# Second layer normalisation written by ScalarE instead of VectorE, and the gate's first step one slot earlier

## The chip, the cores and the metric

One core of a Trainium2 chip runs the whole program. The time is the device time of one execution in microseconds (us); lower is better. The engines are TensorE (PE; its weight loads are shown apart as PEld), VectorE (DVE), ScalarE (ACT), GpSimd (POOL) and the queue engine SyncE (SP). Each runs its own instructions in order, and they wait for one another on semaphores.

## What is computed

2048 rows (tokens) of 128 numbers pass an attention over the context and then a mixture of experts. The reference, cut to what matters:

```python
def layernorm(x): return (x - mean(x)) / sqrt(var(x) + 1e-5)      # along a row

# attention: Wq gives queries, keys and values; 32 x 64 rows are read as one batch of rows
q = layernorm(x) @ Wq.T;  k = v = ctx @ Wq.T
x1 = x + softmax(causal(q @ k.T / sqrt(128))) @ v

# mixture of 8 experts (128 -> 256 -> 128), the two with the highest gate each
xf = layernorm(x1)
gates = softmax(xf @ gate_W)
cw = the two highest gates of a row, scaled to the sum 1; 0 for the others
out = xf + sum over e of cw[:, e] * (relu(xf @ W1[e] + b1[e]) @ W2[e] + b2[e])
result = x1 + out
```

The second layer normalisation, `xf = (x1 - mean) * rstd` with `rstd = (var + 1e-5) ** -0.5`, is what the change touches. In the kernel x1 has a row in each partition, so mean and rstd are one number for each partition and tile.

## The kernel before

**Tiling.** The 2048 rows are 16 tiles of 128 rows, in 4 groups of 4 tiles (groups 0 to 3). The four passes of the main loop, `group(g)`, run the 8 experts over group g, two slots for each expert: slot 2e and slot 2e+1 of pass g. In this document the passes are called first, second, third and fourth (g = 0 to 3). Inside the slots of pass g stands the attention and the gate of the next group, g+1 (and the first half of the attention of g+2), so that group g+1 is ready when its pass begins. The work ahead of the loop (here "the head") does the attention and the gate of group 0 in two halves of two tiles and begins group 1.

**One pass.** In each step e PE first multiplies expert e+1's first layer (`hidden_product`: two column blocks c = 0 and 1, 3 matmuls of 512 columns each, into psH0 and psH1; products of fp16 halves `hi` and `lo`), then does the work of slot 2e, then expert e's second layer (`output_product`, into psY0 or psY1 by turns), then slot 2e+1. ACT follows with `hidden_relu`: for each of psH0 and psH1 an fp16 result h_hi and an fp32 result h (experts 0 and 3 only h). POOL and DVE subtract them for h_lo (`hidden_lo0` for the first block, `hidden_lo` for the second). DVE adds each expert's output, times the gate, to acc (`add_expert`, 4 instructions at L864). A bank psH is free for the next expert when ACT has written its h; a bank psY is free when DVE has added it.

**Order.** A table of numbers gives each helper step the slot of its engine; `run(steps, slot)` calls a step of group a in slot `(a - 2) * 16 + at` of the whole loop, which for steps of group g+1 is slot `at - 16` of pass g. All engines' lists are written out in that order when the program is built. The chain that the change touches, for group g+1 in pass g:
- slot 5: DVE's `variance_step` (statistics of x1, var2), POOL's `attention_rstd` (rstd2, a power of -1/2)
- slot 7 (NORM2 = 23): DVE's `second_norm`, 4 instructions at L784 that write xf
- slot 10 (26): PE transposes xf into psB (`xf_transposes`, L292), ACT evacuates it as fp16 x_hi (`x_hi_part`, L548), DVE writes the rest x_lo (`x_lo_part`, L790), POOL sums x1 and xf into acc (`base_sum`)
- slot 12 (28): PE's `logit_product` (12 small matmuls, L354 to L356, into psD), which waits for x_lo
- slot 13 (29): DVE's `gate_top` (L800 to L808: the logits, the highest of them, `below` = logits less the highest), then ACT's `gate_exps` (exp of below, L553)
- slots 14 and 15: DVE's `gate_choice` and `gate_weights` (L814 to L839).

In the pass that is at expert 7 PE multiplies expert 0 of the next group, and ACT's `hidden_relu` for it stands right behind `gate_exps` in ACT's order. The next `hidden_product` on PE waits for that `hidden_relu`.

In the head the same steps of group 0 run once in halves: DVE's `second_norm` between the statistics of group 1's x and their mean; ACT's `values_out` of group 1 (L527) and then `x_hi_part` (L548); PE's transposes of xf, the score product of group 1 (L333) and the first `hidden_product` in halves (L506 to L508); DVE's mask and maximum of group 1's scores (L741), w1_lo, and `gate_top`.

Of the kernel before, what the change touches and what calls it, by code (L numbers as in the profile page):

```python
# [7 lines left out]
ALU = mybir.AluOpType  # L8
ACT = mybir.ActivationFunctionType
# [24 lines left out]
def xattn_moe(nc, x, ctx, wq, gate_w, w1, b1, w2, b2, out):  # L34
    P = 128
# [4 lines left out]
    TG = 4  # L40
# [30 lines left out]
    with stack:  # L71
        def sb(name, shape, dt=fp32):
            return stack.enter_context(nc.sbuf_tensor(name, shape, dt))
# [4 lines left out]
        def sem(name):  # L78
            return stack.enter_context(nc.semaphore(name))
# [51 lines left out]
        x1 = sb("x1", [P, TG, D])  # L131
        stats2 = sb("stats2", [P, TG, 6])
        mv2 = sb("mv2", [P, TG, 2])
        var2 = sb("var2", [P, TG])
        rstd2 = sb("rstd2", [P, TG])
        xf = sb("xf", [P, TG, D])

        logits = sb("logits", [P, TG, E])
# [28 lines left out]
        LOOP_BANKS = {"xT": psA, "ctxT": psC, "keysT": psB, "values": psC, "scores": psA, "probsT": psB, "attn": psA,  # L167
                      "xfT": psB}
# [4 lines left out]
        ALL = range(TG)  # L173
        HALVES = list(zip((range(0, 2), range(2, 4)), HEAD_BANKS))
# [26 lines left out]
        attn_ps = sem("attn_ps")  # L201
        x1_ready, var2_ready, rstd2_ready = sem("x1_ready"), sem("var2_ready"), sem("rstd2_ready")
        xf_ready, xfT_ps, xhi_ready, xlo_ready = sem("xf_ready"), sem("xfT_ps"), sem("xhi_ready"), sem("xlo_ready")
        base_ready = sem("base_ready")
# [21 lines left out]
        X_OUT, KEYS_OUT, VALUES_OUT, EXPS, PROBS_OUT, X_HI, GATE_EXP = 11, 13, 15, 16, 18, 26, 29  # L226
        STATS, MAX, RESIDUAL, VARIANCE, NORM2, X_LO, GATE_TOP, CHOICE, WEIGHTS = 11, 15, 20, 21, 23, 26, 29, 30, 31
        W1_LO = (3, 0, 2, 5)
# [289 lines left out]
        def _(act):  # L518
# [16 lines left out]
            keys_halves_out = evacuate(keysT, "keysT", keysT_ps, keysT_ready, 1.0 / (SK * SV))  # L535
# [9 lines left out]
            def x_hi_part(a, ts, banks):  # L545
# [3 lines left out]
                                     scale=SX).then_inc(xhi_ready, len(ts))  # L549

            def gate_exps(a):
                act.wait_ge(below_ready, a + 1)
                nc.scalar.activation(gate_exp[:, :, :], below[:, :, :], ACT.Exp).then_inc(gate_exp_ready, 1)  # L553
# [20 lines left out]
            def inputs_out(a):  # L574
# [3 lines left out]

            steps = [(X_OUT, 2, inputs_out), (KEYS_OUT, 2, lambda a: keys_halves_out(a, ALL, LOOP_BANKS)),
                     (VALUES_OUT, 2, lambda a: values_halves_out(a, ALL, LOOP_BANKS)),  # L580
# [52 lines left out]
            keys_out(1, ALL, FIRST_BANKS)  # L633
            values_out(1, ALL, FIRST_BANKS)
            for ts, banks in HALVES:
                x_hi_part(0, ts, banks)
# [88 lines left out]
        def _(dve):  # L725
# [54 lines left out]

            def second_norm(a, ts):
                for t in ts:
                    dve.wait_ge(rstd2_ready, a * TG + t + 1)
                    nc.vector.tensor_scalar(xf[:, t, :], x1[:, t, :], mv2[:, t, 0:1], rstd2[:, t:t + 1],  # L784
                                            ALU.subtract, ALU.mult).then_inc(xf_ready, 1)

# [111 lines left out]
            def wq_lo_part():  # L898
                dve.wait_ge(wq_hi_ready, 2)
                for whole, hi, lo in ((gram, gram_hi, gram_lo), (wqT, wqT_hi, wqT_lo)):  # L900
# [3 lines left out]
            steps = [(CTX_LO, 2, ctx_lo_part), (STATS, 2, statistics), (MAX, 2, lambda a: mask_and_max(a, ALL, banks_of(a))),  # L904
                     (RESIDUAL, 1, residual_step), (VARIANCE, 1, variance_step), (NORM2, 1, lambda a: second_norm(a, ALL)),
                     (X_LO, 1, lambda a: x_lo_part(a, ALL, LOOP_BANKS)), (GATE_TOP, 1, lambda a: gate_top(a, chain)),
# [87 lines left out]
            for ts, banks in HALVES:  # L994
                second_norm(0, ts)
            chain.wait()
# [36 lines left out]
```

## Time and profile before

| | us |
|---|---|
| median of 3 runs (131.57 to 131.89) | 131.86 |
| the profiled execution | 130.83 |
| span of its trace | 129.0 |

| engine | busy us | share of the span | instructions |
|---|---|---|---|
| PE matmul | 120.3 | 93% | 1175 |
| PE weight load | 90.7 | 70% | 1175 |
| DVE | 107.6 | 83% | 419 |
| ACT | 93.5 | 73% | 191 |
| POOL | 53.5 | 41% | 57 |

The granted clock of PE is 1.00 over the whole span (2.4 GHz). The main loop begins at about 21.4 us; the passes end at about 51, 79, 105 and 126.6 us. Busy time counts an instruction from its start to its end, and neighbours on one engine overlap a little; a matmul of 512 fp16 columns lasts 0.38 us and the next one starts 0.22 us after it. So PE's starts tell more than its busy share: where a start comes later than the one before it plus the usual step, PE has lost that time.

### The profile page before, as it was taken

Reading aid. Unit: us, or ns where it says so; the run is one execution under the profiler, and the core shown is the slowest. Engines: PE = TensorE matmul, PEld = TensorE weight load, DVE = VectorE, ACT = ScalarE, POOL = GpSimd, SP = SyncE. Lnnn points to the kernel's source line nnn. Section 1 sums busy time; section 2 is a strip of 40 time slices with the busy share of each in tenths; the row PEclk is TensorE's granted clock in tenths of the full one; section 3 lists DMA queues with packets and bytes.
Section 4 is the critical chain, followed back from the end, with each engine's and each line's share of the span. In section 5 each row is a group of like instructions: output and inputs, shape, how many; then the busy total and the mean of one; then the engine's idle time right before and its main releaser. Section 6 shows DMA issues by size and latency. Waiting matters only on the chain. (4 is left out here: it accounts for less than half of the span.)

```text
span 129.0 us, 3295 instructions
## 1 busy us (share of the span) xinstructions
PE 120.3 (93%) x1175; PEld 90.7 (70%) x1175; DVE 107.6 (83%) x419; ACT 93.5 (73%) x191; POOL 53.5 (41%) x57
## 2 busy tenths in 40 slices
PE   6987788999979999999999999999999979999991
PEld 2585566777847768778768778778776757776690
DVE  0629998989999999989898999958998798866683
ACT  3337485999776955996779927993799467989830
POOL 7199155330094951330095640330468303345400
PEclk9999999999999999999999999999999999999999
DMA  3999900000000000200000000200000002000002
GB/s 92 321 283 321 289 26 8 0 0 0 5 0 0 0 5 3 81 0 5 0 0 5 0 3 13 68 5 0 3 0 8 0 0 86 3 0 0 5 0 81
DMA packets 9904, 5.54 MB, mean 43 GB/s; under 512 B 504, under 2 KB 9888, under 8 KB 9888
## 3 DMA queue, kind: packets, MB, share of 16 engines
q1 hardware_dynamic: 9744, 5.27, 15.2%
q8 instruction: 9, 0.15, 0.5%
q10 hardware_dynamic: 144, 0.07, 0.2%
q14 instruction: 7, 0.06, 0.1%
HBM read 4.28 MB, written 1.05 MB: 41 GB/s over the span
## 5 line engine op out<-in xcount | busy, mean ns | idle before, releaser
L690 POOL TENSOR_TENSOR h_lo<-h,h_hi 128x512 f16<-128x512 f32 x24 | 28.7, 1196 | 40.2 <-ACT h L571 39.9
L571 ACT ACTIVATE h<-psH,b1T 128x512 f32<-128x512 f32 x64 | 43.3, 689 | 1.1 <-PE psH L508 0.9
L570 ACT ACTIVATE h_hi<-psH,b1T 128x512 f16<-128x512 f32 x48 | 33.0, 688 | 11.5 <-PE psH L387 11.4
L864 DVE SCALAR_TENSOR_TENSOR acc<-psY,weight_y,acc 128x128 f32<-128x128 f32 x125 | 35.1, 342 | 1.4 <-PE psY L408 1.2
L383 PE MATMUL psH<-x_hi,w_hi 128*128 128x512 f16 x62 | 23.5, 379 | 1.0 <-ACT h L571 1.0
L387 PE MATMUL psH<-x_lo,w_hi 128*128 128x512 f16 x62 | 23.5, 379 | 0.0
L384 PE MATMUL psH<-x_hi,w_lo 128*128 128x512 f16 x62 | 23.5, 379 | 0.0
L848 DVE TENSOR_TENSOR h_lo<-h,h_hi 128x512 f16<-128x512 f32 x24 | 16.5, 689 | 7.8 <-ACT h L571 7.3
L408 PE MATMUL psY<-w_hi,h_hi 128*128 128x128 f16 x192 | 22.7, 219 | 0.0
L408 PE MATMUL psY<-w_lo,h_hi 128*128 128x128 f16 x192 | 22.7, 219 | 0.0
L408 PEld LDWEIGHTS psY<-w_hi,h_hi 128*128 128x128 f16 x192 | 15.3, 98 | 2.2
L408 PE MATMUL psY<-w_hi,h_lo 128*128 128x128 f16 x192 | 14.6, 219 | 0.8 <-POOL h_lo L690 0.8
L408 PEld LDWEIGHTS psY<-w_sb,h 128*128 128x128 f32 x116 | 14.1, 192 | 1.0
L408 PEld LDWEIGHTS psY<-w_lo,h_hi 128*128 128x128 f16 x192 | 14.7, 98 | 0.0
L408 PE MATMUL psY<-w_sb,h 128*128 128x128 f32 x116 | 14.3, 275 | 0.0
L673 POOL TENSOR_TENSOR rstd<-var,half 128x4 f32<-128x4 f32 (+1 forms) x5 | 4.7, 953 | 21.8 <-DVE var L771 21.8
L408 PEld LDWEIGHTS psY<-w_hi,h_lo 128*128 128x128 f16 x192 | 11.6, 98 | 1.0 <-issue 0.9
L387 PEld LDWEIGHTS psH<-x_lo,w_hi 128*128 128x128 f16 x62 | 6.1, 98 | 7.3
L383 PEld LDWEIGHTS psH<-x_hi,w_hi 128*128 128x128 f16 x62 | 6.1, 98 | 6.9 <-ACT h L571 3.1
L384 PEld LDWEIGHTS psH<-x_hi,w_lo 128*128 128x128 f16 x62 | 6.1, 98 | 2.8
L677 POOL TENSOR_TENSOR rstd<-mv,half 128x4 f32<-128x4 f32 x4 | 5.0, 1250 | 5.8 <-DVE mv L734 5.8
L682 POOL TENSOR_TENSOR acc<-x,xf 128x512 f32<-128x512 f32 x4 | 7.1, 1784 | 0.0
(191 smaller groups left out, 191.4 us busy)
## 6 DMA issues: line engine op xcount, KB each, us to landing
w_sb<-in_L_ffn_W_dram SPq DMA_DIRECT2D x8, 256.0 KB, 4.9
out_dram<-acc SPq DMA_DIRECT2D x3, 256.0 KB, 2.3
x_sb<-in_x_dram SPq DMA_DIRECT2D x2, 256.0 KB, 4.0
ctx_sb<-in_ctx_dram SPq DMA_DIRECT2D x2, 256.0 KB, 4.4
x_sb<-in_x_dram SPq DMA_DIRECT2D x1, 512.0 KB, 7.6
ctx_sb<-in_ctx_dram SPq DMA_DIRECT2D x1, 512.0 KB, 8.5
out_dram<-acc SPq DMA_DIRECT2D x2, 128.0 KB, 1.8
wq_sb<-in_L_xattn_Wq_dram ACTq DMA_DIRECT2D x1, 64.0 KB, 2.8
```

Of the source, the lines that this page charges most:

```text
L383: nc.tensor.matmul(psH[c][:, :], w1_hi[:, e, w], x_hi[:, g, :], start=True, stop=False)
L384: nc.tensor.matmul(psH[c][:, :], w1_lo[:, e, w], x_hi[:, g, :], start=False, stop=False)
L387: nc.tensor.matmul(psH[c][:, :], w1_hi[:, e, w], x_lo[:, g, :], start=False, stop=True).then_inc(z_ps, 1)
L408: last = nc.tensor.matmul(o, hidden[:, C * i + c, t * P:(t + 1) * P], weights[:, e, c, :], start=start and c == 0, stop=stop and c == C - 1)
L570: nc.scalar.activation(h_hi[:, C * (e % 2) + c, :], psH[c][:, :], ACT.Relu, bias=bias, scale=scale)
L571: nc.scalar.activation(h[:, C * (e % 2) + c, :], psH[c][:, :], ACT.Relu, bias=bias, scale=scale).then_inc(h_ready, 1)
L673: nc.gpsimd.tensor_tensor(rstd2[:, v], var2[:, v], half[:, v], ALU.pow).then_inc(rstd2_ready, len(ts))
L677: nc.gpsimd.tensor_tensor(rstd[:, bass.ts(a, TG)], mv[:, bass.ts(a, TG), 1], half[:, 0:TG], ALU.pow).then_inc(rstd_ready, TG)
L682: nc.gpsimd.tensor_tensor(acc[:, bass.ts(a, TG), :], x1[:, :, :], xf[:, :, :], ALU.add).then_inc(base_ready, 1)
L690: nc.gpsimd.tensor_tensor(h_lo[:, i, :], h[:, i, :], h_hi[:, i, :], ALU.subtract).then_inc(hlo0_ready, 1)
L848: nc.vector.tensor_tensor(h_lo[:, i, :], h[:, i, :], h_hi[:, i, :], ALU.subtract).then_inc(hlo_ready, 1)
L864: last = nc.vector.scalar_tensor_tensor(out=o, in0=y, scalar=weight_y[:, g % 2, t, e:e + 1], in1=o, op0=ALU.mult, op1=ALU.add)
```

## The change

xf is no longer written by DVE as `(x1 - mean) * rstd` but by ACT as `Identity(rstd * x1 + shift2)`, with `shift2 = -mean * rstd` as a bias of one number for each row and rstd2 as a scale of one number for each row. DVE keeps one small instruction for each group that writes shift2 (two in the head, one for each half), in slot 6 instead of 7 (NORM2 = 22). ACT's 4 instructions stand in slot 8 (NORM_ACT = 24), that is behind `hidden_relu` of expert 5 and ahead of that of expert 6; in the head they stand behind `values_out` of group 1 and ahead of `x_hi_part`. And GATE_TOP goes from 29 to 28: DVE does `gate_top` ahead of `add_expert` of expert 6 instead of behind it.

```diff
@@ sizes and semaphores @@
+        shift2 = sb("shift2", [P, TG])
+        shift2_ready = sem("shift2_ready")
@@ -224,7 +226,8 @@
-        STATS, MAX, RESIDUAL, VARIANCE, NORM2, X_LO, GATE_TOP, CHOICE, WEIGHTS = 11, 15, 20, 21, 23, 26, 29, 30, 31
+        NORM_ACT = 24
+        STATS, MAX, RESIDUAL, VARIANCE, NORM2, X_LO, GATE_TOP, CHOICE, WEIGHTS = 11, 15, 20, 21, 22, 26, 28, 29, 31
@@ ACT @@
+            def second_norm(a, ts):
+                act.wait_ge(shift2_ready, a * TG + ts[-1] + 1)
+                for t in ts:
+                    nc.scalar.activation(xf[:, t, :], x1[:, t, :], ACT.Identity, bias=shift2[:, t:t + 1],
+                                         scale=rstd2[:, t:t + 1]).then_inc(xf_ready, 1)
-            steps = [(X_OUT, 2, inputs_out), (KEYS_OUT, 2, lambda a: keys_halves_out(a, ALL, LOOP_BANKS)),
+            steps = [(X_OUT, 2, inputs_out), (NORM_ACT, 1, lambda a: second_norm(a, ALL)), (KEYS_OUT, 2, lambda a: keys_halves_out(a, ALL, LOOP_BANKS)),
@@ -632,6 +641,8 @@
             values_out(1, ALL, FIRST_BANKS)
+            for ts, banks in HALVES:
+                second_norm(0, ts)
             for ts, banks in HALVES:
                 x_hi_part(0, ts, banks)
@@ DVE @@
-            def second_norm(a, ts):
-                for t in ts:
-                    dve.wait_ge(rstd2_ready, a * TG + t + 1)
-                    nc.vector.tensor_scalar(xf[:, t, :], x1[:, t, :], mv2[:, t, 0:1], rstd2[:, t:t + 1],
-                                            ALU.subtract, ALU.mult).then_inc(xf_ready, 1)
+            def second_shift(a, ts):
+                v = slice(ts[0], ts[-1] + 1)
+                dve.wait_ge(rstd2_ready, a * TG + ts[-1] + 1)
+                nc.vector.scalar_tensor_tensor(out=shift2[:, v], in0=mv2[:, v, 0], scalar=-1.0, in1=rstd2[:, v],
+                                               op0=ALU.mult, op1=ALU.mult).then_inc(shift2_ready, len(ts))
-                     (RESIDUAL, 1, residual_step), (VARIANCE, 1, variance_step), (NORM2, 1, lambda a: second_norm(a, ALL)),
+                     (RESIDUAL, 1, residual_step), (VARIANCE, 1, variance_step), (NORM2, 1, lambda a: second_shift(a, ALL)),
@@ -992,7 +1003,7 @@
             for ts, banks in HALVES:
-                second_norm(0, ts)
+                second_shift(0, ts)
```

CHOICE goes from 30 to 29, too; in DVE's order `gate_choice` stands between `add_expert` of expert 6 and that of expert 7 in both kernels.

**ACT in the head.** The copies out of the first attention of group 1 and the fp16 copy of group 0's xf, before (line numbers are those of each kernel):

```order
L527 ACTIVATE keysT<-psY1 128x512 [waits keysT_ps]
L527 ACTIVATE values<-psC 128x512 [waits values_ps]
L548 ACTIVATE x_hi<-psD 128x256 [waits xfT_ps]
L548 ACTIVATE x_hi<-psB 128x256 [waits xfT_ps]
L520 ACTIVATE w1_hi<-w1_sb 128x512 [waits w1_in2,b1_ready]
```

and after:

```order
L530 ACTIVATE keysT<-psY1 128x512 [waits keysT_ps]
L530 ACTIVATE values<-psC 128x512 [waits values_ps]
L557 ACTIVATE xf<-x1,shift2,rstd2 128x128 [waits shift2_ready]
L557 ACTIVATE xf<-x1,shift2,rstd2 128x128
L557 ACTIVATE xf<-x1,shift2,rstd2 128x128 [waits shift2_ready]
L557 ACTIVATE xf<-x1,shift2,rstd2 128x128
L551 ACTIVATE x_hi<-psD 128x256 [waits xfT_ps]
L551 ACTIVATE x_hi<-psB 128x256 [waits xfT_ps]
L523 ACTIVATE w1_hi<-w1_sb 128x512 [waits w1_in2,b1_ready]
```

Four new instructions stand between the copy of the values and x_hi.

**ACT in the third pass.** The end of `hidden_relu` of expert 5, that of expert 6, and x_hi of group 3, before:

```order
L570 ACTIVATE h_hi<-psH1,b1T 128x512 [waits z_ps]
L571 ACTIVATE h<-psH1,b1T 128x512
L570 ACTIVATE h_hi<-psH0,b1T 128x512 [waits z_ps]
L571 ACTIVATE h<-psH0,b1T 128x512
L570 ACTIVATE h_hi<-psH1,b1T 128x512 [waits z_ps]
L571 ACTIVATE h<-psH1,b1T 128x512
L548 ACTIVATE x_hi<-psB 128x512 [waits xfT_ps]
```

and after:

```order
L579 ACTIVATE h_hi<-psH1,b1T 128x512 [waits z_ps]
L580 ACTIVATE h<-psH1,b1T 128x512
L557 ACTIVATE xf<-x1,shift2,rstd2 128x128 [waits shift2_ready]
L557 ACTIVATE xf<-x1,shift2,rstd2 128x128 x3
L579 ACTIVATE h_hi<-psH0,b1T 128x512 [waits z_ps]
L580 ACTIVATE h<-psH0,b1T 128x512
L579 ACTIVATE h_hi<-psH1,b1T 128x512 [waits z_ps]
L580 ACTIVATE h<-psH1,b1T 128x512
L551 ACTIVATE x_hi<-psB 128x512 [waits xfT_ps]
```

The relus of expert 6 and x_hi stand behind the four instructions that write xf; the first and second pass have the same order.

**DVE in the third pass.** From the second subtraction of expert 7 (h_lo) to the gate's choice, before:

```order
L848 TENSOR_TENSOR h_lo<-h,h_hi 128x512 [waits h_ready]
L864 SCALAR_TENSOR_TENSOR acc<-psY0,weight_y,acc 128x128 [waits y_used,y_ps]
L864 SCALAR_TENSOR_TENSOR acc<-psY0,weight_y,acc 128x128 x3
L800 TENSOR_SCALAR logits<-psD 128x32 [waits logits_ps]
L803 MAX top8<-logits 128x8 [waits dve_chain]
L803 MAX top8<-logits 128x8 x3
L805 TENSOR_TENSOR below<-logits,top8 128x32 [waits dve_chain]
L806 TENSOR_TENSOR is_second<-logits,top8 128x32
L807 TENSOR_TENSOR one_above<-top8 128x4
L808 TENSOR_TENSOR above<-logits,top8 128x32
L814 SCALAR_TENSOR_TENSOR nth<-restart,is_second 128x32 [waits dve_chain]
```

and after:

```order
L859 TENSOR_TENSOR h_lo<-h,h_hi 128x512 [waits h_ready]
L811 TENSOR_SCALAR logits<-psD 128x32 [waits logits_ps]
L814 MAX top8<-logits 128x8 [waits dve_chain]
L814 MAX top8<-logits 128x8 x3
L816 TENSOR_TENSOR below<-logits,top8 128x32 [waits dve_chain]
L817 TENSOR_TENSOR is_second<-logits,top8 128x32
L818 TENSOR_TENSOR one_above<-top8 128x4
L819 TENSOR_TENSOR above<-logits,top8 128x32
L875 SCALAR_TENSOR_TENSOR acc<-psY0,weight_y,acc 128x128 [waits y_used,y_ps,dve_chain]
L875 SCALAR_TENSOR_TENSOR acc<-psY0,weight_y,acc 128x128 x3
L825 SCALAR_TENSOR_TENSOR nth<-restart,is_second 128x32
```

The first step of the gate now stands ahead of the four additions of expert 6.

## Rows read from the trace of the kernel before

**Rows 1.** Busy by stage (span; PE, PEld, DVE, ACT, POOL; clock; DMA), second and third pass

```profile
51.00:99.30 48.30, 48.30 (x487) 37.11 (x484) 43.65 (x167) 39.27 (x80) 19.11 (x16) 1.00 0.04 13
```

**Rows 2.** Timeline (start, duration, engine, line, what, [idle before]), PE, end of third pass

```profile
99.09 0.38 PE L387 MATMUL psH<-x_lo,w_hi 128*128 128x512 f16 x1
99.59 0.18 PE L354 MATMUL psD<-gate_hi,x_hi 128*128 128x8 f16 x1
...
103.43 0.61 PE L408 MATMUL psY<-w_hi,h_lo 128*128 128x128 f16 x8
104.76 0.38 PE L383 MATMUL psH<-x_hi,w_hi 128*128 128x512 f16 x1 [0.72 <-ACT h L571]
```

**Rows 3.** Timeline, ACT, third pass from the last relu of expert 5

```profile
94.82 0.70 ACT L571 ACTIVATE h<-psH,b1T 128x512 f32<-128x512 f32 x1
95.78 0.69 ACT L570 ACTIVATE h_hi<-psH,b1T 128x512 f16<-128x512 f32 x1 [0.26 <-PE psH L387]
...
98.86 0.69 ACT L570 ACTIVATE h_hi<-psH,b1T 128x512 f16<-128x512 f32 x1 [0.17 <-PE psH L387]
...
103.81 0.23 ACT L553 ACTIVATE gate_exp<-below 128x32 f32<-128x32 f32 x1 [2.53 <-DVE below L805]
103.94 1.25 ACT L571 ACTIVATE h<-psH,b1T 128x512 f32<-128x512 f32 x2
```

**Rows 4.** Timeline, DVE, third pass

```profile
94.28 1.95 DVE L784 TENSOR_SCALAR xf<-x,mv,rstd 128x128 f32<-128x128 f32 x4
...
98.24 0.69 DVE L848 TENSOR_TENSOR h_lo<-h,h_hi 128x512 f16<-128x512 f32 x1 [0.37 <-ACT h L571]
...
101.92 1.12 DVE L864 SCALAR_TENSOR_TENSOR acc<-psY,weight_y,acc 128x128 f32<-128x128 f32 x4
102.95 0.18 DVE L800 TENSOR_SCALAR logits<-psD 128x32 f32<-128x32 f32 x1
```

**Rows 5.** ACT's prices: groups by line and form (busy, mean ns), then one from the timeline

```profile
L571 ACT ACTIVATE h<-psH,b1T 128x512 f32<-128x512 f32 x64 | 43.3, 689 | 1.1 <-PE psH L508 0.9 <-PE psH L387 0.2
L542 ACT ACTIVATE probs<-neg_s,neg_max 128x128 f32<-128x128 f32 x16 | 6.2, 406 | 0.8 <-DVE neg_max L741 0.8
L520 ACT ACTIVATE ctx_hi<-psC 128x512 f16<-128x512 f32 x2 | 1.2, 597 | 0.0
```

```profile
31.89 0.33 ACT L520 ACTIVATE gram_hi<-gram 128x128 f16<-128x128 f32 x1
```

**Rows 6.** Timeline, ACT in the first and second pass, PE in the second

```profile
39.99 0.69 ACT L570 ACTIVATE h_hi<-psH,b1T 128x512 f16<-128x512 f32 x1 [1.13 <-PE psH L387]
...
66.94 0.70 ACT L571 ACTIVATE h<-psH,b1T 128x512 f32<-128x512 f32 x1
```

```profile
68.35 0.60 PE L292 MATMUL psB<-ident,xf 128*128 128x128 f32 x4
...
72.09 0.38 PE L387 MATMUL psH<-x_lo,w_hi 128*128 128x512 f16 x1
```

**Rows 7.** Timeline, the head: DVE, then ACT, then PE

```profile
16.72 1.10 DVE L784 TENSOR_SCALAR xf<-x,mv,rstd 128x128 f32<-128x128 f32 x4
...
19.99 0.35 DVE L741 CUSTOM_DVE_ANT_0 neg_s<-psA,mask,rstd 128x128 f32<-128x128 f32 x1 [0.34 <-POOL rstd L677]
```

```profile
17.11 0.60 ACT L527 ACTIVATE values<-psC 128x512 f32<-128x512 f32 x1 [0.29 <-PE psC L309]
```

```profile
18.04 1.06 PE L333 MATMUL psA<-keysT,xT 128*128 128x128 f32 x8
```

**Rows 8.** Timeline, POOL, DVE and PE: the gate's weights beside POOL's subtraction

```profile
53.16 1.16 POOL L690 TENSOR_TENSOR h_lo<-h,h_hi 128x512 f16<-128x512 f32 x1 [4.22 <-ACT h L571]
```

```profile
53.19 1.17 DVE L825 TENSOR_TENSOR chosen<-chosen,gate_exp 128x32 f32<-128x32 f32 x1
...
109.02 0.69 DVE L848 TENSOR_TENSOR h_lo<-h,h_hi 128x512 f16<-128x512 f32 x1 [0.26 <-DVE weight_cat L839]
```

```profile
110.02 0.61 PE L408 MATMUL psY<-w_hi,h_lo 128*128 128x128 f16 x8
```

## The prediction

> **What bounds the kernel now.** I read the busy table by stage first, then the starts on PE, and then what ACT and DVE do where PE starts late. In the second and third pass PE is busy for 48.30 of 48.30 us, DVE for 43.65 and ACT for 39.27 [rows 1]. So nothing is to be had from a shorter DVE unless PE waits for it, and of PE's waits the change can only touch those behind xf, x_lo and the gate. The starts show two, both at the end of the third pass [rows 2]. The first gate matmul starts at 99.59, where 99.09 plus the usual 0.22 makes 99.31: 0.28 us lost, waiting for x_lo. The next first-layer product starts at 104.76. Eight matmuls of 0.056 us behind 103.43 end the issue at 103.86, so 0.90 us are lost, waiting for ACT's h of expert 0. ACT began that h at 103.94, right behind gate_exp, which had waited 2.53 us for DVE's below [rows 3]; DVE began the gate at 102.95, behind the additions of expert 6 [rows 4]. The first two passes have PE work (the scores of the group after next) in that place and lose nothing there. So the most that the new place of the gate can bring is 0.90 us, once.
>
> **The price of the new ACT work.** No instruction on ACT in the trace has both a scale and a bias for each row. Three neighbours bound it [rows 5]. A copy of 128 elements from SBUF, with neither, takes 0.33 us. The exp of 128 elements from SBUF, with a bias for each row, takes 0.41 us. The copy of 512 elements out of PSUM takes 0.597 and the relu of the same size with a bias for each row 0.689, so one operand for each row costs 0.092 us. A second one makes 0.406 + 0.092 = 0.50 us. The step to the next is less: two relus take 1.25 us where one takes 0.69 [rows 3, 5], so the second starts 0.12 us before the first ends, and instructions of 0.50 us start 0.38 to 0.39 us apart. That is my value: xf's last tile is written 3 x 0.39 + 0.50 = 1.67 us after the first starts, and ACT is held for 4 x 0.39 = 1.56 us. It is the middle row plus the same step again, so I take it over the lower ends, which are 0.41 (only the bias costs, step about 0.3) and 0.33 (nothing costs, step 0.21 to 0.24). The upper end adds nothing more than 0.05 us each, as the spread of the copies from SBUF and PSUM.
>
> That a scale for each row costs as much as a bias is in no row here. The Trainium skill says it, in "ScalarE: Activation LUTs", section "What ACT_TABLE_LOAD costs": an ACTIVATE with immediates takes 186 ns plus 0.833 ns for each element, each operand of one number for each row adds about 93 ns, and neighbours overlap by about 93 ns. An estimate from that page is 0.48 us and a step of 0.39 us, against 0.50 and 0.39 above; the sum by it would be smaller by less than 0.1 us. The trace agrees on the bias with its 0.092 us.
>
> **What the parts do, in time order.**
>
> Head. DVE writes xf from 16.72 to 17.82 [rows 7]. Now ACT can start only behind the copy of the values, which starts at 17.11 as PE delivers them and leaves ACT free at 17.61. The last xf is ready at 17.61 + 1.67 = 19.28 instead of 17.82: 1.46 us later. PE's last transpose and with it the scores of group 1 (18.04) go to about 19.44 to 19.50, and end 1.06 us later, at 20.5. DVE's mask and maximum waited until 19.99 for POOL's rstd, a cover of about 0.9 us; they now start at 20.55, 0.56 us later. The other branch, x_hi and x_lo of the second half, ends at the same time. Behind the mask DVE is without a gap up to the gate's first step, and gate_exp, the relus of expert 1 and the softmax on ACT follow it: the loop begins 0.56 us later. With the prices 0.41 and 0.33 it is +0.2 and 0. DVE's own saving of 1 us there is worth nothing, since all that follows waits for ACT. The shift2 instructions, 2 of some 0.17 us, fit where xf was written.
>
> First pass. Ahead of the relus of expert 6 at 39.99 ACT is idle for 1.13 us, waiting for PE [rows 6]; the four instructions lie in that gap but for 0.4 us. The remaining 0.4 us is covered by PE's transposes of x and the context. Zero. The waits of PE in this pass, for POOL's and ACT's earlier steps, stay.
>
> Second pass. The relu of expert 5 that starts at 66.94 leaves ACT free at 67.51 [rows 6]. The last xf is ready at 69.18. PE's four transposes of xf start at 68.35, 0.11 us apart, the last at 68.68: now at 69.22, a loss of 0.55 us. The relus of expert 6 start at 67.51 + 1.56 = 69.07 instead of 67.91, 1.16 us later, and with them x_hi, the subtraction for h_lo and x_lo. That would bring the gate matmuls to 72.87; PE, late by 0.55, comes there at 72.09 + 0.22 + 0.55 = 72.86. So the two delays are one: +0.55 us. Prices 0.41 and 0.33 make it +0.24 and 0.
>
> Third pass. ACT is free at 95.39, behind the relu at 94.82 [rows 3]; xf ends at 97.06, again 0.54 us late for the transposes. The relus of expert 6 start at 96.95 instead of 95.78. DVE's h_lo at 98.24 already waits for them [rows 4], x_lo follows it, and PE already waits for x_lo: the whole 1.17 us arrives at the gate matmuls, 100.76 instead of 99.59. PE then reaches the product where it lost 0.90 us at 103.86 + 1.17 = 105.03. The h that it needs: the relus of expert 7 are late by about 1.0 us (1.17 less the 0.17 that they waited at 98.86), so is DVE's h_lo behind them; the gate no longer stands behind the additions, which saves 102.95 - 101.92 = 1.03 us. The gate therefore begins at about the old time, and h is there at about 104.7, before PE. The 0.90 us wait is gone, but only because PE comes later: 105.03 against 104.76, +0.27 us. With the price 0.41 the delay is 0.85 us and the balance -0.05; with 0.33 it is 0.57 and the balance -0.32.
>
> Fourth pass: no step of the change is in it. DVE's 1.95 us for xf in each pass [rows 4] goes away, the shift2 of some 0.17 us comes in behind h_lo of expert 4; it needs rstd2, which POOL has delivered by then, and behind it only additions with 2 us to spare are queued. ACT's wait for shift2 ends over 1 us before ACT comes to it. No DMA is moved, and SP's stores wait for additions that PE does not wait for.
>
> **Sum.** 0.56 + 0 + 0.55 + 0.27 = 1.38 us. On the profiled execution's own time that is 130.83 + 1.38 = 132.2 (its span 129.0 to 130.4). The profiled execution lies 1.03 us under the median of the runs; the sum on the median is 131.86 + 1.38 = 133.2 us, 1.0% slower.
>
> **The rivals.**
>
> A: ACT's instructions are cheap, and the kernel is not slower. This is the other side, and one number decides it: the step from one xf to the next on ACT. At the copy's price the sum is 0 + 0 + 0 - 0.32: 131.5 us. The balance is zero at a step of about 0.28 us. For it speaks only that a scale might cost nothing; against it, that the exp with its bias alone already is at 0.41 us. Chance 0.12.
>
> B: only the bias costs (0.41 us, step 0.3): 0.2 + 0.24 - 0.05 = +0.4, 132.3 us. Chance 0.2.
>
> C: DVE's lateness meets POOL. Where POOL's subtraction runs, DVE's small product of two SBUF tiles took 1.17 us (53.16 and 53.19, [rows 8]) and not the 0.18 of DVE's small instructions (102.95, [rows 4]). In the fourth pass the subtraction for h_lo of expert 1 starts at 109.02, ends at 109.71, and PE reads it at 110.02: 0.3 us to spare. In the changed kernel DVE comes to the gate's weights up to 1 us later and may meet POOL with the first product, not with a later one; what follows the first one takes 0.7 us more. Then PE waits 0.4 us there: +1.8, 133.7 us. It decides from 0.3 us of extra lateness. Chance 0.18.
> The Trainium skill, in "SBUF — State Buffer", section "SBUF: two separate sides", has the rule: a DVE instruction with two SBUF inputs and a GpSimd one that reads SBUF exclude each other for a whole instruction. By that rule the new shift2 instruction (two small SBUF inputs) would be held as well, for up to 1 us behind POOL's subtraction of expert 4, with time to spare before ACT wants it; the 1.17 us agrees with it.
>
> **Chances and range.** Forecast 0.5, A 0.12, B 0.2, C 0.18. The forecast's own range, from the transposes' and the head's margins of 0.2 us each and 0.05 us more for each ACT instruction, is 132.7 to 133.7. The range for 8 in 10 takes in most of B and C: 131.9 to 133.9. A measurement of this kernel tells about 0.3% (0.4 us) from no change. Faster by more than that needs A and a little more: 0.07. Within it: the rest of A, and half of B, and something for a head that hides more than I see: 0.2. Slower: 0.73.
>
> **What the new profile would show.** Right: ACT's xf instructions last 0.48 to 0.52 us; PE's transposes of xf in the second and third pass start with gaps; the gate matmuls of the third pass start about 1.2 us late against their pass; no wait of PE for h at the start of the fourth pass; DVE with some 6 us less busy time and more idle time waiting for ACT's h; the first scores mask in the head near 20.5. Wrong: xf instructions of 0.33 to 0.4 us, or transposes of xf without gaps. The prediction fails most easily if ACT's new instructions overlap more than the relus do, or if the head's 0.56 us disappears in the waits at the start of the first pass.

## The result, and the profile after

The changed kernel takes 134.76 us in the median of six runs (133.04 to 135.90); the kernel before, beside it, took 131.74 us (131.19 to 131.98). Three of the six lie at 135.9, because TensorE's clock falls to half in the head of those executions (below); the ratios in this text compare the executions in which it doesn't. That ratio is 1.0123, 95% interval 1.0085 to 1.0161: 1.6 us slower. A second set of six gave 1.0144 (1.0105 to 1.0184), 1.9 us. With the falls in the count, the first six are 3.0 us over before in the median (134.76 against 131.74), which is outside the foretold range of 131.9 to 133.9; only the executions without a fall are in it.

The profiled execution is one of those at 135.86 us (span 134.1). Busy times of its page, and its row of TensorE's granted clock, in 40 slices of 3.35 us:

```profile
PE 124.0 (92%) x1175; PEld 92.7 (69%) x1175; DVE 106.7 (80%) x408; ACT 99.0 (74%) x207; POOL 52.3 (39%) x57
...
PEclk9999995899999999999999999999999999999998
```

ACT has 16 instructions and 5.5 us more than before (93.5), as meant. DVE, which lost 16 instructions of xf, has only 0.9 us less than its 107.6. And the clock of the seventh slice, the head's end, has the digit 5 (0.5 of full speed); the kernel before has a 9 (0.9 or more) in every slice.

The new instructions (groups by line and form: busy, mean ns of one), which answer to the prices in [rows 5]. The second row stands for DVE's three instructions of shift2 in the passes:

```profile
L557 ACT ACTIVATE xf<-x,shift,rstd 128x128 f32<-128x128 f32 x16 | 6.6, 495 | 0.0
L795 DVE SCALAR_TENSOR_TENSOR shift<-mv,rstd 128x4 f32<-128x4 f32 x3 | 3.4, 1119 | 0.0
```

The end of the third pass (timeline, the engines side by side), which answers to [rows 2], [rows 3] and [rows 4]:

```profile
100.20 1.65 ACT L557 ACTIVATE xf<-x,shift,rstd 128x128 f32<-128x128 f32 x4
101.04 1.19 PE L295 MATMUL psB<-ident,xf 128*128 128x128 f32 x4
101.73 0.69 ACT L579 ACTIVATE h_hi<-psH,b1T 128x512 f16<-128x512 f32 x1
104.19 0.69 DVE L859 TENSOR_TENSOR h_lo<-h,h_hi 128x512 f16<-128x512 f32 x1 [2.10 <-ACT h L580]
105.53 0.18 PE L357 MATMUL psD<-gate_hi,x_hi 128*128 128x8 f16 x1 [0.51 <-DVE x_lo L801]
107.59 0.18 DVE L811 TENSOR_SCALAR logits<-psD 128x32 f32<-128x32 f32 x1
108.44 0.23 ACT L562 ACTIVATE gate_exp<-below 128x32 f32<-128x32 f32 x1 [1.49 <-DVE below L816]
109.82 0.38 PE L386 MATMUL psH<-x_hi,w_hi 128*128 128x512 f16 x1
```

ACT's four instructions take 1.65 us; the relu behind them starts 1.53 after the first. DVE waits 2.10 us for the h that follows, x_lo and the gate matmuls come late, and the first-layer product at 109.82 has no wait left, where before it had lost 0.90 us: PE now comes there later itself.

The clean way to say where the time went is by stage. Below, the head runs from the first value product (`psC<-wqT,ctxT`) to the first full-precision output product (`psY<-w_sb,h`), and each pass from one such output product to the next, the last to the end of the span. The load ahead of the value product lands at 15.85 to 17.0 us, by chance, in any of the kernels, so spans alone mislead by up to 1.1 us. The table is worked out from the timelines, one execution for each row; e1 is the changed kernel once more, in an execution whose clock stays at 1.00:

| us | value product at | head | pass 1 | pass 2 | pass 3 | pass 4 |
|---|---|---|---|---|---|---|
| before | 15.96 | 6.81 | 29.49 | 27.88 | 25.91 | 22.95 |
| after | 17.00 | 9.27 | 30.21 | 28.47 | 26.17 | 22.98 |
| after again (e1) | 15.85 | 7.71 | 30.23 | 28.47 | 26.18 | 22.96 |
| foretold | | +0.56 | 0 | +0.55 | +0.27 | 0 |
| e1 less before | | +0.90 | +0.74 | +0.59 | +0.27 | +0.01 |

The second, third and fourth pass are as foretold. The head and the first pass are not, and neither is the 1.56 us by which the head of the profiled execution is longer than that of e1.

One entry of the table has to be read with care. The passes repeat within a few hundredths of a us wherever a kernel has the same steps in them, and the head with ScalarE's xf does too where the clock stays at 1.00 (7.70 to 7.73 us in four traces). The head with DVE's xf doesn't: in the seven traces that have it (before and six of the kernels below) it takes 6.81 to 7.24 us, and before's is the shortest. PE waits there for DVE's xf for 0 to 0.53 us; in the trace of the gate's move alone, for example,

```profile
17.90 0.58 PE L292 MATMUL psD<-ident,xf 128*128 128x128 f32 x2 [0.52 <-DVE xf L784]
```

where before has no such wait. So ScalarE's place in the head costs between 0.47 and 0.90 us there, and +0.90 is the upper end.

### The profile page after: what moved, and what is told of

It is laid out like the page before. It is cut to its first block and busy times, and to the rows that moved or that the text cites. A ratio compares the mean times of both kernels' runs of the same rounds, so it can differ in the third digit from the quotient of the medians.

```text
span 134.1 us, 3305 instructions
## 1 busy us (share of the span) xinstructions
PE 124.0 (92%) x1175; PEld 92.7 (69%) x1175; DVE 106.7 (80%) x408; ACT 99.0 (74%) x207; POOL 52.3 (39%) x57
## 5 line engine op out<-in xcount | busy, mean ns | idle before, releaser
L580 ACT ACTIVATE h<-psH,b1T 128x512 f32<-128x512 f32 x64 | 43.8, 697 | 2.2 <-PE psH L511 2.0
L545 ACT ACTIVATE probs<-neg_s,neg_max 128x128 f32<-128x128 f32 x16 | 6.2, 405 | 0.8 <-DVE neg_max L752 0.8
```

The lines of the kernel that those rows point to most:

```text
L545: nc.scalar.activation(probs[:, t, :], neg_s[:, t, :], ACT.Exp, bias=neg_max[:, t:t + 1], scale=-1.0, accum_out=row_sum[:, t:t + 1]).then_ ...
L580: nc.scalar.activation(h[:, C * (e % 2) + c, :], psH[c][:, :], ACT.Relu, bias=bias, scale=scale).then_inc(h_ready, 1)
```

## The experiments

Three theories stand behind them: that PE's wait for xf in the head lets the clock fall; that ACT's price of 0.5 us for each xf makes the delays of the second and third pass; and that DVE, whose work has moved against before, meets POOL, and one holds the other.

### The changed kernel again

> The changed kernel unchanged, for more executions and another profile. In the first profile the granted clock fell to 0.50 for 3.4 us in the head, right behind the place where PE waited 1.1 us for xf. Theory T1 (the wait in the head brings the clock down in some executions, and the rest is ACT's price): the times fall into two groups, one near 133.2 us with the clock near 1.0 over the head and one near 135.9 us with 0.50 for some 3 us; the first is 1.4 to 1.6 us over the kernel before. Theory T2 (the clock fall is an accident of the chip that has nothing to do with the change): it shows as often in the kernel before, and not at the same place.

133.18, 133.01, 133.89 and 133.63 us, and twice 135.8: the same two levels. The lower ones have a mean clock of 0.997 or more, the upper ones 0.985 and 0.987. None of the 20 executions of the kernel before that ran beside them is at such a clock, which speaks against an accident that has nothing to do with the change. What the fall looks like, in the profiled execution (timeline of PE):

```profile
17.00 1.05 PE L312 MATMUL psC<-wqT,ctxT 128*128 128x128 f32 x8
19.18 0.71 PE L295 MATMUL psD<-ident,xf 128*128 128x128 f32 x2 [1.13 <-ACT xf L557]
19.95 0.71 PE L295 MATMUL psB<-ident,xf 128*128 128x128 f32 x2
20.49 1.69 PE L336 MATMUL psA<-keysT,xT 128*128 128x128 f32 x8
21.98 0.42 PE L509 MATMUL psH<-x_hi,w_hi 128*128 128x256 f16 x1
```

and in e1, at 1.00 throughout:

```profile
18.03 0.71 PE L295 MATMUL psD<-ident,xf 128*128 128x128 f32 x2 [1.13 <-ACT xf L557]
18.80 0.71 PE L295 MATMUL psB<-ident,xf 128*128 128x128 f32 x2
19.35 1.06 PE L336 MATMUL psA<-keysT,xT 128*128 128x128 f32 x8
20.25 0.27 PE L509 MATMUL psH<-x_hi,w_hi 128*128 128x256 f16 x1
```

Up to the transposes the two are equal, with the same wait of 1.13 us. Then eight score products take 1.69 us instead of 1.06, and a product of 256 columns 0.42 instead of 0.27. Busy time by stretch (the first columns are span, PE, PEld, DVE, ACT, POOL, then the granted clock), of the profiled execution:

```profile
18.00:20.50 2.50, 1.21 (x6) 0.59 (x5) 1.49 (x9) 2.35 (x6) 1.52 (x2) 1.00 0.01 3
20.50:24.00 3.50, 3.50 (x19) 2.88 (x19) 2.62 (x11) 1.46 (x4) 1.49 (x2) 0.54 0.02 7
```

PE was busy for 1.21 of 2.50 us at full clock; then it runs for about 3.4 us at 0.50, that is 1.2 GHz instead of 2.4.

### The gate's move alone

```
-         ... GATE_TOP, CHOICE, WEIGHTS = ... 29, 30, 31
+         ... GATE_TOP, CHOICE, WEIGHTS = ... 28, 29, 31      (in the kernel before)
```

> The kernel before with only the new place of the gate's first step (GATE_TOP 28, CHOICE 29); the second normalisation stays on VectorE in slot 7. By the prediction's reading the gate only removes PE's wait of 0.90 us at the start of the fourth pass: 0.9 us faster, about 130.9 us, and PE has no gap at that product. Rival: the additions of expert 6 that now come behind the gate are needed, and the gain is under 0.3 us.

Ratio 0.9948 (0.9918 to 0.9977): 0.7 us faster. The third pass takes 25.04 instead of 25.91 us, so 0.87 of the 0.90 us are there. But the fourth takes 23.21 instead of 22.95: DVE's small instruction at line 828 falls beside POOL's subtraction and takes 0.69 us, where its neighbours take 0.16 to 0.19.

```profile
106.88 1.21 POOL L690 TENSOR_TENSOR h_lo<-h,h_hi 128x512 f16<-128x512 f32 x1 [4.70 <-ACT h L571]
106.89 0.18 DVE L825 TENSOR_TENSOR chosen<-chosen,gate_exp 128x32 f32<-128x32 f32 x1
107.42 0.69 DVE L828 SCALAR_TENSOR_TENSOR sum_two<-sum_all,sum_two 128x4 f32<-128x4 f32 x1
```

### The head's normalisation back on DVE

The changed kernel, with the four xf of the head written by DVE as before; the three passes keep ACT.

```
-             for ts, banks in HALVES:
-                 second_norm(0, ts)          (ACT's program, the head)
...
-                 second_shift(0, ts)         (DVE's program, the head)
+                 second_norm_dve(0, ts)
```

> The changed kernel, but the second normalisation of the head (group 0) is done by VectorE as before; in the loop ScalarE does it. If ACT's place in the head is what brings the clock down and costs the rest of the head, the executions form one group with clock 1.0, and only the loop's cost is left: the passes were 0.72, 0.59, 0.26 and 0.03 us longer in the trace of the changed kernel, together 1.6 us, so 133.3 us if all of the loop's cost stays, and no execution near 135.9. If the clock fall is an accident, some executions are still at 135 or more.

The ratio is 1.0128 (1.0093 to 1.0164), with no fall of the clock in six executions. Its head is 6.90 us, nearly before's, but its first pass is 30.55, which is 1.06 us longer than before's. So the first pass has a loss of its own, which the foretold "zero" missed, and in the changed kernel the head's delay covers 0.3 us of it.

### Only the head's normalisation on ACT

The reverse, in the kernel before: shift2 and ACT's four instructions in the head, nothing else.

> The kernel before, but the second normalisation of the head is done by ScalarE with scale and bias for each row; the loop and the gate are as before. By the prediction +0.56 us (132.3 us). With the clock fall, a second group of executions some 2.4 us later than that, and the mean clock near 0.985 in them. If the head's delay is covered in executions without the clock fall, they are within 0.3 us of the kernel before.

By the trace the head is 0.92 us longer and the first pass 0.32 shorter: +0.60, against 0.56 foretold. The executions without a fall have a ratio of only 1.0007 (0.9981 to 1.0033), 0.1 us. A part of the difference is before's short head: against the trace of the gate's move alone, which has the same steps in the head and the first pass as before, the two together are only 0.15 us longer (36.90 against 36.75). In 4 of 12 runs the mean clock is 0.987 and the time 133.8 us.

### The wait in the head filled

The changed kernel, with six products of the warming-up tile in PE's wait, into a bank that is free there. The same kernel ran again later, for more executions.

```
+             for _ in range(FILL):                              (FILL = 6)
+                 nc.tensor.matmul(psH[0][:, :], warm[:, 0:P], warm[:, :], start=True, stop=True)
              for ts, banks in HALVES:
                  xf_transposes(0, ts, banks)
```

> The changed kernel with 6 matmuls of 512 columns (products of zeros that nobody reads, 1.3 us) on PE in the head, in the place where it waits for xf from ScalarE. They do nothing but keep PE busy. Theory T1 (PE's wait there is what the clock falls after): no execution has the clock at 0.50 in the head, all are near 133.3 us, none near 135.8. Rival (what matters is how late the head is, or ScalarE's work): the second group of executions stays, with 5 of 12 at 135.8 as in the changed kernel.

> The version with the 6 matmuls of zeros in the head again (e5_fill), only for more executions: with T1 again none near 135.8 us; the two together would make it 0 of 12 where 3 of 8 is the share without them. If the first 6 were chance, 2 or 3 of 6 are near 135.8.

No fall of the clock in 12 executions. PE's timeline in the second set:

```profile
17.61 1.46 PE L502 MATMUL psH<-warm 128*128 128x512 f16 x6
18.90 0.71 PE L296 MATMUL psD<-ident,xf 128*128 128x128 f32 x2
19.67 0.71 PE L296 MATMUL psB<-ident,xf 128*128 128x128 f32 x2
20.22 1.06 PE L337 MATMUL psA<-keysT,xT 128*128 128x128 f32 x8
```

The fill takes nothing (head 7.70 against 7.71 us in e1, all passes as in e1). The ratios are 1.0153 (1.0102 to 1.0204) and 1.0175 (1.0131 to 1.0220).

### A late normalisation on DVE

The kernel before, with ACT untouched: DVE writes the head's xf behind the mean and variance and one weight conversion, so that PE waits for it.

```
-             for ts, banks in HALVES:
-                 second_norm(0, ts)
              chain.wait()
              mean_and_var(TG, 2 * TG, chain)
              w2_lo_part(0)
+             for ts, banks in HALVES:
+                 second_norm(0, ts)
```

> The kernel before, but in the head VectorE writes xf behind the mean of group 1's x and behind w2_lo, some 1.2 us later. ScalarE has no new work; only PE's wait for xf grows, to about 1.2 us. Theory T1 (the clock falls after PE's wait, whoever causes it): some executions have the clock at 0.50 for about 3 us in the head (mean clock 0.985 to 0.987, 2.4 us longer), as in the versions with ScalarE's xf in the head (9 of 24 so far). Rival (ScalarE's work or its position is what matters): no such execution in 6 or more, as in the kernel before (0 of 40).

PE waits 1.74 us, and in 5 of 12 executions the mean clock is 0.987 and the time 133.7 to 134.1 us; the others take 131.4 to 132.0, a ratio of 1.0018 (0.9985 to 1.0050). PE's timeline, then the busy time by stretch as above:

```profile
19.48 0.58 PE L292 MATMUL psD<-ident,xf 128*128 128x128 f32 x2 [1.74 <-DVE xf L784]
19.99 0.73 PE L292 MATMUL psB<-ident,xf 128*128 128x128 f32 x2
20.52 1.92 PE L333 MATMUL psA<-keysT,xT 128*128 128x128 f32 x8
```

```profile
18.00:20.00 2.00, 0.52 (x3) 0.29 (x3) 1.89 (x10) 0.43 (x1) 1.52 (x2) 1.00 0.02 4
20.00:21.00 1.00, 1.00 (x6) 0.92 (x6) 0.54 (x2) 0.56 (x2) 0.76 (x2) 0.50 0.00 0
```

So it is PE's long wait that makes the fall frequent, whoever makes PE wait, and filling the wait takes the fall away. It isn't the only thing that can: the next two experiments (e7 and e6) have one fall each, in 12 and in 6 executions, with xf in the head written by DVE and waits of 0.35 and 0.53 us in their traces.

### The first pass: one DVE step moved out of POOL's way

The kernel with the head back on DVE, and the conversion of gram and wqT to their low halves (line 912 of the changed kernel) two slots sooner.

```
-         WQ_HI, WQ_LO, CTX_LO = 5, 9, 11
+         WQ_HI, WQ_LO, CTX_LO = 5, 7, 11
```

> The version with the head on VectorE (e3_head_dve), with the two subtractions gram_lo and wqT_lo of the first pass two slots sooner (WQ_LO 7 instead of 9). In the changed kernel they took 1.15 and 1.35 us instead of 0.28 each, while GpSimd's h_lo and the sum of x1 and xf ran, and PE then waited 1.1 us for x_lo. Theory T3 (exclusion of VectorE and GpSimd at SBUF costs the first pass its 1.06 us): they take 0.3 us each or little more, PE does not wait for x_lo in the first pass, the first pass is 29.5 us as before instead of 30.55, and the kernel is 1.0 us faster than e3_head_dve. Rival (x_lo is late there because of ScalarE's relus, as in the third pass): the first pass keeps at least 0.7 us of its loss.

The first pass takes 29.46 us instead of 30.55; before's is 29.49. The ratio falls from 1.0128 to 1.0043 (1.0008 to 1.0078), 1.1 us, where 1.0 was expected. Two of the 12 executions are not in it: one with a mean clock of 0.987 (134.81 us), and one of 134.09 us at a clock of 1.00, which has no explanation. The timelines show why. The changed kernel, DVE and POOL, and the gate matmuls that come late:

```profile
44.78 1.16 POOL L701 TENSOR_TENSOR h_lo<-h,h_hi 128x512 f16<-128x512 f32 x1 [1.95 <-ACT h L580]
45.91 1.31 POOL L693 TENSOR_TENSOR acc<-x,xf 128x512 f32<-128x512 f32 x1
...
44.94 1.15 DVE L912 SCALAR_TENSOR_TENSOR gram_lo<-gram,gram_hi 128x128 f16<-128x128 f32 x1
46.01 1.35 DVE L912 SCALAR_TENSOR_TENSOR wqT_lo<-wqT,wqT_hi 128x128 f16<-128x128 f32 x1
47.29 0.68 DVE L859 TENSOR_TENSOR h_lo<-h,h_hi 128x512 f16<-128x512 f32 x1
...
48.63 0.18 PE L357 MATMUL psD<-gate_hi,x_hi 128*128 128x8 f16 x1 [0.92 <-DVE x_lo L801]
```

The kernel before, where DVE came first and POOL was the one that took longer:

```profile
42.67 0.28 DVE L901 SCALAR_TENSOR_TENSOR gram_lo<-gram,gram_hi 128x128 f16<-128x128 f32 x1
42.70 2.20 POOL L682 TENSOR_TENSOR acc<-x,xf 128x512 f32<-128x512 f32 x1
42.87 0.28 DVE L901 SCALAR_TENSOR_TENSOR wqT_lo<-wqT,wqT_hi 128x128 f16<-128x128 f32 x1
```

And the experiment, ahead of POOL's subtraction:

```profile
39.83 0.29 DVE L916 SCALAR_TENSOR_TENSOR gram_lo<-gram,gram_hi 128x128 f16<-128x128 f32 x1
40.04 0.28 DVE L916 SCALAR_TENSOR_TENSOR wqT_lo<-wqT,wqT_hi 128x128 f16<-128x128 f32 x1
```

Two instructions of 0.28 us took 1.15 and 1.35 us when they started 0.1 to 0.2 us behind one of POOL's. That is 1.9 us of DVE, behind which stand h_lo and x_lo, and PE loses 1.09 us at the gate matmuls. The recorded rival, that ACT's relus make x_lo late there, would have left at least 0.7 us of the loss in place; nothing of it is left.

### The scale taken off the instruction

The same kernel as in the third experiment, with `scale=1.0` for `scale=rstd2[:, t:t + 1]`; it leaves the multiplication by rstd out, so only its times mean something.

> The version with the head on VectorE (e3_head_dve), but ScalarE's instructions for xf have the scale 1.0 in place of the operand for each row; xf is then not the normalised value, and what follows from it changes with it. Only the price is asked. If the operand for the scale costs 0.09 us: the instruction takes 0.40 to 0.41 us instead of 0.496, ScalarE is held for 1.2 us instead of 1.54, and the second and third pass are 0.3 us shorter each than in e3_head_dve (28.47 and 26.17 us). If a second operand is free, nothing changes.

One instruction takes 411 ns instead of 500, so the second operand costs 0.09 us, the same as the first. The first and second pass become 0.28 and 0.37 us shorter; the second, at 28.10 us, is 0.22 over before, where the prediction's working gave 0.24 for this price. But the third becomes 0.77 longer: now DVE's h_lo and POOL's sum start in the same instant, and h_lo is the one that is held.

```profile
100.75 1.81 DVE L863 TENSOR_TENSOR h_lo<-h,h_hi 128x512 f16<-128x512 f32 x1 [1.74 <-ACT h L580]
100.75 1.26 POOL L691 TENSOR_TENSOR acc<-x,xf 128x512 f32<-128x512 f32 x1
```

The price is as foretold; the sum isn't proportional to it, since each new order makes collisions of its own. The ratio is 1.0102 (1.0051 to 1.0154). One execution of six had a mean clock of 0.987.

### The gate put back in the changed kernel

> The changed kernel with the gate's first step back behind the additions of expert 6 (GATE_TOP 29, CHOICE 30). By the prediction's reading PE comes to the start of the fourth pass at about the time when h is ready only because the gate was moved: without that, h is 1.0 us later and PE waits about 0.7 us. So the third pass is 26.85 us instead of 26.17 and the executions without the clock fall are near 133.9. Rival (the gate's move gives nothing where ScalarE is late): less than 0.3 us.

Line 229 again has GATE_TOP 29 and CHOICE 30. The third pass takes 26.78 us instead of 26.17, since the first-layer product waits for h once more (lost: 0.62 us):

```profile
109.50 0.23 ACT L562 ACTIVATE gate_exp<-below 128x32 f32<-128x32 f32 x1 [2.53 <-DVE below L816]
110.45 0.38 PE L386 MATMUL psH<-x_hi,w_hi 128*128 128x512 f16 x1 [0.44 <-ACT h L580]
```

So the gate's move is worth 0.6 us in the changed kernel (0.7 expected). In 4 of 6 executions the clock fell; the other two take 133.9 and 134.3 us, a ratio of 1.0200 (1.0129 to 1.0270).

### A better version: the gate's move and POOL's rstd

The trace of before has one more loss of PE in the first pass: 0.91 us, waiting for POOL's h_lo, which stands behind POOL's rstd. The gate's move alone, and that step one slot later:

```
-         FIRST_RSTD, RSTD, BASE = 12, 21, 26
+         FIRST_RSTD, RSTD, BASE = 12, 22, 26
```

> A try for a version that is faster than both: e2_gate_only (normalisation on VectorE, gate's first step one slot sooner) and GpSimd's rstd2 one slot later (RSTD 22), behind its subtraction for expert 4 and not ahead of it. In the first pass PE loses 0.91 us at 37.67 waiting for that subtraction, which stood behind rstd2. Expected: that loss is gone, 0.9 us less than e2_gate_only, about 129.7 us; the rival is that xf then comes late for PE's transposes, with a gain under 0.3 us.

The ratio is 0.9899 (0.9864 to 0.9934), 130.3 us against 131.75: the lowest ratio of all, 1.0% below before. Against the gate's move alone the first pass takes 28.86 instead of 29.52 us, and the fourth gives 0.45 of it back (23.66 against 23.21): DVE meets POOL with its first small product. So the rstd step brings less than the 0.9 us expected, 0.2 by the traces and 0.6 by the ratios, whose intervals (0.9918 to 0.9977 for the gate alone) overlap.

```profile
106.44 1.16 POOL L690 TENSOR_TENSOR h_lo<-h,h_hi 128x512 f16<-128x512 f32 x1 [4.65 <-ACT h L571]
106.50 1.15 DVE L825 TENSOR_TENSOR chosen<-chosen,gate_exp 128x32 f32<-128x32 f32 x1
...
110.20 0.62 PE L408 MATMUL psY<-w_hi,h_lo 128*128 128x128 f16 x8 [0.52 <-DVE h_lo L848]
```

With the gate's weights a slot later (WEIGHTS 32 instead of 31):

> A second try for a faster version: e8_gate_and_rstd with the gate's weights one slot later (WEIGHTS 32), behind VectorE's h_lo of expert 1. In e8's trace the first product of the weights met GpSimd's subtraction and took 1.15 us, that h_lo came late and PE lost 0.69 us at 110.20 in the fourth pass. Expected: that loss is gone, 0.6 us less than e8, near 1.5% under the kernel before. Rival: the additions of expert 0, which now come behind the weights, hold psY0 back and PE waits there instead.

A miss, and the rival on record isn't what happened either. The fourth pass takes 23.79 us. DVE's h_lo is in time now, but the last step of the weights meets POOL's next subtraction, and PE loses 0.85 us ahead of the transposes of the weights (at 110.66):

```profile
109.38 1.18 POOL L690 TENSOR_TENSOR h_lo<-h,h_hi 128x512 f16<-128x512 f32 x1 [1.92 <-ACT h L571]
109.58 1.03 DVE L839 SCALAR_TENSOR_TENSOR weight_cat<-weight,weight_cat 128x32 f16<-128x32 f32 x1
```

The ratio is 0.9941 (0.9908 to 0.9974), with one execution of 206 us at a clock of 0.57 left out, for which there is no explanation.

## Why the prediction was right, and where not

**What bounds it.** Right. PE is the bound, and the gate's whole worth is the 0.90 us at the end of the third pass. Alone it brings 0.87 there (e2), in the changed kernel 0.6 (e11).

**ACT's price.** Right: 0.495 us against 0.50, the next 0.385 us later against 0.38 to 0.39. That a scale for each row costs what a bias costs, which no row of before showed, is shown by e6 (0.411 us without it, 0.500 with it). Rivals A and B fall with it.

**Second and third pass.** Right: +0.59 and +0.27 against 0.55 and 0.27. PE's four transposes of xf in the second pass start over 1.02 us, where 0.44 is their own time. In the third, against the start of the pass, the gate matmuls are 1.13 us later (foretold 1.17) and the first-layer product of the fourth pass 0.25 (0.27), with its wait gone. So the 1.17 us of delay and the 0.90 us of vanished wait, which nearly cancel, were each right.

**The head.** Its sum is within what the traces allow, the path was not right. The step that let the loop begin with DVE's mask has the mask itself right: in e4 it starts 0.59 us late (foretold 0.56). But PE is the later one. Its score products start 1.42 us late as foretold; before, the next first-layer product waited for x_lo and started 1.42 us behind them (18.04 to 19.46), now it follows after 0.90. So PE leaves the head 0.90 us late, and waits in the first pass give 0.32 back: 0.58 against the profiled execution of before, which the prediction was worked out on, and less against a head of before that is longer (down to 0.15, if it is 7.24 us). That 0.58 is so near to 0.56 is partly luck.

**The first pass.** Wrong, and the largest miss: "zero" measured 1.06 us without the head's delay and 0.74 with it. The step that failed counted only ACT's four instructions and what they push; it left DVE's new times out. DVE has lost 1.95 us of xf there and got back 1.1 for shift2, so its next steps stand at other times beside POOL's, and two of them are held (+1.9 us); moving these two out of POOL's way gives the 1.06 us back (e7). That is rival C's mechanism, in the first pass and not in the fourth, where C had put it. In the fourth DVE did meet POOL (line 839, 0.92 us at 112.27 in the profiled execution), but PE lost nothing by it: +0.01 us.

**Shift2 and DVE's busy time.** 0.17 us was the estimate for shift2 in the passes, 1.12 us was measured. The sentence on rival C had named this possibility: it starts at 40.62 while POOL's subtraction, from 40.23, runs.

```profile
40.23 2.60 POOL L701 TENSOR_TENSOR h_lo<-h,h_hi 128x512 f16<-128x512 f32 x2
40.62 1.11 DVE L795 SCALAR_TENSOR_TENSOR shift<-mv,rstd 128x4 f32<-128x4 f32 x1
```

The foretold sign of "some 6 us less busy time" on DVE failed by the same mechanism: it is 0.9 us. Of the 7.0 us of xf, 3.7 come back as shift2 (1.12 us three times, and the head's), 2.0 in gram_lo and wqT_lo, and 1.2 in the small products of line 839, which were held more often; other small steps were held less.

The Trainium skill, in "SBUF — State Buffer", section "SBUF: two separate sides", has the rule for both: of a DVE instruction with two SBUF inputs and a GpSimd one that reads SBUF, whichever starts first has the shared port pair for the whole instruction, and the other is blocked. The traces agree, down to an instruction of four columns (1.12 us). The prediction had weighed it for shift2 and for the fourth pass, and had not asked it of every DVE instruction that the change moves.

**The clock.** Not foreseen. The prediction had PE wait over 1 us in the head and charged only the wait. In 13 of the 30 executions of kernels with that wait (the changed kernel 3 of 6 and 2 of 6, e4 4 of 12, e11 4 of 6) the clock fell, in 5 of 12 of e9, in none of 12 with the wait filled, and in none of the kernel before, of which over 60 ran beside them. It costs 1.56 us in the head (9.27 against 7.71).

The rest of the 2.4 us between the two levels is probably the load: in the three traces with a fall (after, e9, e11) the value product starts at 16.7 to 17.0, in e1 and e4, which have the long wait and no fall, at 15.9. The late load alone brings no fall: with the wait filled it starts at 16.7 and 16.9, and with DVE's xf at 17.0 (e3), all at a clock of 1.00. The times fit. The falls of the changed kernel, less the 1.56 us, lie at 134.2 to 134.3 us; six of the 12 executions with the wait filled lie at 134.0 to 134.5, and none of the seven of the changed kernel without a fall is over 133.9. So those without a fall seem to be the ones with an early load, and a comparison that keeps only them reads low. That would explain why the filled kernel, which has no falls, shows 2.0 and 2.3 us where the changed one shows 1.6 and 1.9. No run set the time of the load, so it isn't shown, and why a late load should matter is open.

**The total.** 1.38 us were foretold and 1.6 to 1.9 measured; the stages of e1 add up to 2.5, the profiled execution of before being a low one of its kind. With the other heads of the seven traces in place of before's (6.81 to 7.24 us) they add up to 2.1 to 2.5, and the 2.0 and 2.3 us of the filled kernel, the one comparison that loses no execution to the clock, fit that. So the change costs 2.0 to 2.5 us without a fall and the total of 1.38 came out low; it came near because the missed term is 0.7 us and not more, and because the executions without a fall read low. The single falls in e6 and e7, where the wait in the head is at most 0.53 us, stay open.

## What to carry to other kernels

Moving work off an engine that was not the bound gained nothing here and cost what it delayed elsewhere: the 0.5 us instructions on ACT stand ahead of relus that PE needs, and DVE's saved time turned into waiting, for ACT's h and for POOL. When a change shifts an engine against another that shares SBUF with it, list every instruction with two SBUF inputs in the shifted stretch and look what the other engine runs there. And a new wait of PE over 1 us, where none was, is to be charged with a possible fall of the clock as well, or filled with products that nobody needs. Last, a stage of the kernel before is to be read from more than one execution before a difference of 0.5 us is taken from it.

## What the runs showed of the hardware

- With a wait of PE of 1.13 us in the head (1.74 in e9) the granted clock fell in 13 of 30 (5 of 12) executions; in the three traces of such executions it went from 1.00 to 0.50 behind the wait, in that of the changed kernel for about 3.4 us. Six products of 512 columns in the wait, which cost no time, kept it at 1.00 in 12 of 12.
- A DVE instruction with two SBUF inputs that starts behind a tensor_tensor of POOL lasts until about that one's end: 1.11 us for four columns, 1.15 us for 128x128 whose own time is 0.28. If DVE is first, POOL's is the longer one: 2.20 us for the sum that takes 1.31 elsewhere. Started in the same instant, DVE's h_lo took 1.81 instead of 0.69 us and POOL's sum its usual 1.26. A hundredth of a us can decide: line 825 at 106.89, beside POOL's subtraction from 106.88, took 0.18 us (e2), at 106.50 beside one from 106.44 it took 1.15 (e8).
- ACT: each operand with one number for each row costs 0.09 us, scale and bias alike (0.689 against 0.597 us for 512 elements with and without a bias; 0.500 against 0.411 for 128 with bias and scale and with the bias alone).
